# Experts of a recurrent and mixture-of-experts block: gate and up products with the weights stationary, and a second matrix split 128 + 64

## The reference, cut to what matters

```python
topk_w, selected = jax.lax.top_k(softmax(x @ gate.T), 8)
flat_experts = selected.reshape(-1)
gather_indices = jnp.argsort(flat_experts, stable=True)
x_perm = x[gather_indices // 8]                                   # 16384 rows of 256
first_gemm = ragged_dot(x_perm, swapaxes(gate_up_proj, 1, 2), token_counts)      # 256 -> 384
intermediate = silu(first_gemm[:, :192]) * first_gemm[:, 192:]
second_gemm = ragged_dot(intermediate, swapaxes(down_proj, 1, 2), token_counts)  # 192 -> 256
unperm = zeros_like(second_gemm).at[gather_indices].set(second_gemm)
out = (unperm.reshape(-1, 8, 256) * topk_w[..., None]).sum(axis=1)
```

## Time and profile before

| | us |
|---|---|
| time, median of 3 runs (lowest to highest) | 2985.74 (2984.24 to 2986.35) |
| the profiled execution's own time | 2986.55 |
| its span, first to last instruction | 2985.2 |
| experts' stage, first L902 to last L939 | 2169.7 to 2625.5 |

### The profile page before, as it was taken

How to read it: one execution, slowest core, us unless ns; L and a number is a source line. 1 busy time by engine, 2 the same in 40 slices (tenths; PEclk the granted TensorE clock), 3 DMA queues, 4 the chain that set the end, 5 groups by cost and what they waited for, 6 DMA issues and landing times.

```text
span 2985.2 us, 150990 instructions
## 1 busy us (share of the span) xinstructions
PE 2734.0 (92%) x59732; PEld 2284.0 (77%) x59732; DVE 2077.2 (70%) x12188; ACT 1613.8 (54%) x8443; POOL 338.9 (11%) x457
## 2 busy tenths in 40 slices
PE   7689999999999999999999999998679999979984
PEld 4478999989989899998999989878556666744331
DVE  6688888877777777777777777665456666665238
ACT  3445555566666666666666666543335555511115
POOL 0000101101001010010100101001024444410000
PEclk7555555555555555555555555555589999979997
DMA  3142323212123221231212312101568665251000
GB/s 132 39 118 84 98 73 93 88 38 82 59 75 97 61 83 58 76 92 59 85 55 76 95 57 89 32 14 45 211 222 259 196 193 170 74 175 53 1 0 28
DMA packets 170143, 270.95 MB, mean 91 GB/s; under 512 B 23353, under 2 KB 125644, under 8 KB 167140
## 3 DMA queue, kind: packets, MB, share of 16 engines
q1 hardware_dynamic: 125524, 202.29, 21.6%
q0 software_dynamic: 15312, 33.67, 3.3%
q10 hardware_dynamic: 28608, 25.35, 3.1%
HBM read 170.77 MB, written 98.70 MB: 90 GB/s over the span
## 4 chain that ended last, share of the span: by engine, by line
PE 84%; DVE 8%; ACT 4%; issue 2%; DMA 1%; SPq 0%; POOL 0%; POOLq 0%; ACTq 0%; DVEq 0%
PE work L678 9%; PE bank_h L688 7%; PE bank_r L688 7%; PE bank_z L688 7%; PE bank_g L688 7%; PE bank_h L697 5%; PE work L688 5%; PE bank_r L697 4%; PE bank_z L697 3%; PE bank_g L697 3%; PE work L914 3%; PE bank_z L914 3%; PE bank_h L939 2%; PE work L939 2%; PE work L1025 2%
## 5 line engine op out<-in xcount | busy, mean ns | idle before, releaser
L688 PEld LDWEIGHTS work<-h_run,hi_r 128*128 128x128 f16 x4092 | 258.3, 119 | 164.8 <-DVE h_run L1783 150.0
L688 PE MATMUL work<-h_run,hi_r 128*128 128x2 f16 x4092 | 286.8, 174 | 65.3 <-DVE h_run L1783 60.9
L1783 DVE TENSOR_TENSOR_SCAN h_run<-z_run,hh_run 128x12 f16<-128x12 f32 x1024 | 186.8, 182 | 229.3 <-ACT hh_run L1224 210.5
L1224 ACT ACTIVATE hh_run<-bank_h 128x4 f32<-128x4 f32 x1024 | 179.2, 175 | 275.7 <-PE bank_h L697 275.0
L1205 ACT ACTIVATE r_guess<-work 128x4 f32<-128x4 f32 x1023 | 177.0, 173 | 236.0 <-PE work L688 218.7
L1768 DVE TENSOR_TENSOR_SCAN rh_run<-r_run,h_run 128x12 f16<-128x12 f32 x1023 | 187.1, 183 | 151.5 <-ACT r_run L1214 107.9
L688 PE MATMUL bank_g<-h_hi,hi_g 128*128 128x2 f16 x4092 | 253.4, 166 | 38.7 <-ACT h_hi L1194 38.1
L697 PE MATMUL bank_h<-rh_run,hi_h 128*128 128x2 f16 x4092 | 263.8, 169 | 1.8 <-DVE rh_run L1768 1.2
L1219 ACT ACTIVATE z_run<-bank_z 128x4 f32<-128x4 f32 x1024 | 180.3, 176 | 149.1 <-PE bank_z L697 4.2
L688 PE MATMUL bank_h<-h_run,hi_h 128*128 128x2 f16 x4092 | 253.7, 166 | 3.3 <-DVE h_run L1765 3.3
L697 PE MATMUL bank_g<-h_lo,hi_g 128*128 128x2 f16 x4092 | 253.2, 166 | 1.4 <-DVE h_lo L1746 0.5
(11 more groups left out here) (481 smaller groups left out, 8076.8 us busy)
## 6 DMA issues: line engine op xcount, KB each, us to landing
stage<-in_gate_up SPq DMA_DIRECT2D x128, 384.0 KB
stage<-in_down SPq DMA_DIRECT2D x128, 192.0 KB, 3.0
gu_split<-parts SPq DMA_DIRECT2D x64, 384.0 KB, 2.8
gu_ring<-gu_split SPq DMA_DIRECT2D x64, 384.0 KB
xt<-x_rows ACTq DMA_DIRECT2D x191, 128.5 KB, 2.2
x_rows<-zero_rows SPq DMA_DIRECT2D x64, 257.0 KB, 3.3
yk<-y_rows SPq DMA_DIRECT2D x16, 1024.0 KB, 4.8
dn_split<-parts SPq DMA_DIRECT2D x64, 192.0 KB, 2.7
```

What stands on the lines that cost most here:

```text
L688: ins = pe.matmul(o[:, m, step, :], w[:, k, m * P:(m + 1) * P], hi(k), start=False, stop=False, skip_group_check=True)
L1224: act.activation(two(t.hh_run[:, :, 1]), gate_in(t.h, c2, s2), ACT.Tanh, scale=scale_of["h"]).then_inc(s.hh_act, 1)
L1783: dve.tensor_tensor_scan(t.h2_run[:, 0:3 * KH * B], threes(t.z_run), threes(t.hh_run), 0.0, ALU.mult, ALU.add).then_inc(s.h2hi, 1)
```

## The change

1. **Gate and up.** The weights of the ring become the stationary operand, the turned rows the streamed one. The product comes out with the inner features on the partitions. 384 outputs make three blocks of 128 columns of the bank, so there are 18 matmuls of 128 streamed columns in place of 6 of 384. The host orders the outputs so that block 0 is gate 0:128, block 1 is up 0:128, and block 2 has up 128:192 in its first 64 rows and gate 128:192 in its last 64.
2. **The transposes of `mid`, ACT's copy `midT` and their turn of the loop go**; the loop runs to `NTILES + 1`, and the second matrix is applied in turn i - 2.
3. **ACT** makes `silu` in two instructions; the second reads rows 64:128 of block 2 and writes rows 0:64. **DVE** makes one multiply of 256 columns to single precision, a copy to half precision, and the difference; rows 64:128 of `silu`'s second half stay zero from two memsets.
4. **Second matrix**: 128 and 64 rows of contraction in place of 96 and 96, still six matmuls of 256 streamed columns. Each transfer of an odd piece (stage, split store, ring) becomes two.

```diff
@@ tensor_experts
-    for i in range(NTILES + 3):
+    for i in range(NTILES + 2):
...
-            for q, (a, b) in enumerate(PRODUCTS):
-                for k in range(KH):
-                    w = t.gu_ring[:, bass.ds(slot_of[n], 1), a, k, :].rearrange("p a n -> p (a n)")
-                    ins = pe.matmul(bank[:, 0:2 * INTER], t.xtT[n % 2][:, b, k], w, start=(q == 0 and k == 0),
-                                    stop=(q == 2 and k == KH - 1))
+            for m in range(3):
+                for q, (a, b) in enumerate(PRODUCTS):
+                    for k in range(KH):
+                        w = t.gu_ring[:, bass.ds(slot_of[n], 1), a, k, m * P:(m + 1) * P].rearrange("p a n -> p (a n)")
+                        ins = pe.matmul(bank[:, m * P:(m + 1) * P], w, t.xtT[n % 2][:, b, k], start=(q == 0 and k == 0),
+                                        stop=(q == 2 and k == KH - 1), skip_group_check=True)
             ins.then_inc(s.gu_mm, 1)
...
         n = i - 2
-        if 0 <= n < NTILES:
-            bank = tile_banks(t, n)[2].bitcast(FP16)
+        if n >= 0:
+            bank = tile_banks(t, n)[3]
             pe.wait_ge(s.mid, n + 1)
             if n >= 2:
-                pe.wait_ge(s.midT, n - 1)
-            for part in range(2):
-                for j in range(2):
-                    at = (2 * part + j) * P
-                    ins = pe.transpose(bank[0:HI, at:at + P], t.mid[n % 2][:, part, j * HI:(j + 1) * HI], t.identh)
-            ins.then_inc(s.mid_turned, 1)
-        n = i - 3
...
                 pe.wait_ge(s.yt, n - 1)
-            for q, (a, b) in enumerate(PRODUCTS):
-                for j in range(2):
-                    w = t.dn_ring[:, bass.ds(slot_of[n], 1), a, j, :].rearrange("p a n -> p (a n)")
-                    ins = pe.matmul(bank[:, 0:D], t.midT[n % 2][:, b, j], w, start=(q == 0 and j == 0),
-                                    stop=(q == 2 and j == 1))
+            for j, rows in enumerate((slice(0, P), slice(0, REST))):
+                for q, (a, b) in enumerate(PRODUCTS):
+                    w = t.dn_ring[rows, bass.ds(slot_of[n], 1), a, j, :].rearrange("p a n -> p (a n)")
+                    ins = pe.matmul(bank[:, 0:D], t.mid[n % 2][rows, b, j * P:(j + 1) * P], w, start=(j == 0 and q == 0),
+                                    stop=(j == 1 and q == 2))
             ins.then_inc(s.tiles_done, 1)
@@ scalar_experts
-            act.activation(t.silu[n % 2], tile_banks(t, n)[1][:, 0:INTER], ACT.Silu, scale=t.gu_down).then_inc(s.silu, 1)
+            if n >= 2:
+                act.wait_ge(s.mid, n - 1)
+            act.activation(silu[:, 0:P], bank[:, 0:P], ACT.Silu, scale=t.gu_down)
+            act.activation(silu[0:REST, P:2 * P], bank[REST:P, 2 * P:3 * P], ACT.Silu,
+                           scale=t.gu_down[REST:P]).then_inc(s.silu, 1)
         n = i - 2
-        if 0 <= n < NTILES:
-            act.wait_ge(s.mid_turned, n + 1)
-            if n >= 2:
-                act.wait_ge(s.tiles_done, n - 1)
-            act.copy(t.midT[n % 2].rearrange("p a j n -> p (a j n)"),
-                     tile_banks(t, n)[2].bitcast(FP16)[0:HI, 0:4 * P]).then_inc(s.midT, 1)
@@ vector_experts
-            dve.scalar_tensor_tensor(t.mid[n % 2][:, 0], up, t.gu_mid, t.silu[n % 2], ALU.mult, ALU.mult)
-            v.on(dve.scalar_tensor_tensor(t.mid32[n % 2], up, t.gu_mid, t.silu[n % 2], ALU.mult, ALU.mult))
+            v.on(dve.scalar_tensor_tensor(mid32, tile_banks(t, n)[1][:, P:3 * P], t.gu_mid, t.silu[n % 2], ALU.mult,
+                                          ALU.mult))
             dve.wait_ge(v.sem, v.n)
-            dve.tensor_tensor(t.mid[n % 2][:, 1], t.mid32[n % 2], t.mid[n % 2][:, 0], ALU.subtract).then_inc(s.mid, 1)
+            if n >= 2:
+                dve.wait_ge(s.tiles_done, n - 1)
+            v.on(dve.tensor_copy(mid[:, 0], mid32))
+            dve.wait_ge(v.sem, v.n)
+            dve.tensor_tensor(mid[:, 1], mid32, mid[:, 0], ALU.subtract).then_inc(s.mid, 1)
@@ sync_program
     def fetch_expert(e):
...
-        sp.dma_start(t.dn_ring[:, e % RING].rearrange("p j k n -> p (j k n)"), t.dn_split[e]).then_inc(expert_sem(s, e), 16)
+        sp.dma_start(t.dn_ring[:, slot, :, 0], dn[0:P]).then_inc(expert_sem(s, e), 16)
+        sp.dma_start(t.dn_ring[0:REST, slot, :, 1], dn[P:INTER]).then_inc(expert_sem(s, e), 16)
```

More of the change, by code:

```diff
@@ L40 @@
 NT = NTC * P
-HI = INTER // 2
+REST = INTER - P
 RING = 6
@@ L113 @@
     count_mm table_in table_mm row_table table_sb tiles_done experts_ready tile_ready
-    x_turned xT gu_mm silu mid mid_turned midT yt
+    x_turned xT gu_mm silu mid yt
     tl0 tl1 tl2 tl3 tl4 tl5 tl6 tl7 tl8 tl9 tl10 tl11
@@ L403, in place_tiles @@
                 t.xtT = [sb(f"xtT{i}", [P, 2, KH, P], FP16) for i in range(2)]
[L404 to L407, removed]
+                t.silu = [sb(f"silu{i}", [P, 2 * P]) for i in range(2)]
+                t.mid32 = [sb(f"mid32_{i}", [P, 2 * P]) for i in range(2)]
+                t.mid = [sb(f"mid{i}", [P, 2, 2 * P], FP16) for i in range(2)]
                 t.yt = [sb(f"yt{i}", [P, D]) for i in range(NB)]
@@ L457 @@
 chunk_rows = lambda h2: h2.rearrange("p t (k b) three -> p k t b three", k=KH)[:, :, :, :, 2]
-piece_rows = lambda q: P if q % 2 == 0 else HI
 piece_cols = lambda q: KH * 2 * INTER if q % 2 == 0 else 2 * D
+slice_rows = lambda q, i: slice(0, REST if (q % 2, i) == (1, 1) else P)
 slice_cols = lambda i: slice(i * SLICE, (i + 1) * SLICE)
-piece_view = lambda t, q: t.stage[q % NSTAGE][0:piece_rows(q), 0:piece_cols(q)]
+piece_view = lambda t, q: t.stage[q % NSTAGE][:, 0:piece_cols(q)]
+moves = lambda q: 16 * (1 + q % 2)
 stage_sem = lambda s, q: (s.stage0, s.stage1, s.stage2, s.stage3)[q % NSTAGE]
 store_sem = lambda s, q: (s.store0, s.store1, s.store2)[q % NSPLIT]
-stores_before = lambda q: len([p for p in range(NPIECE, q) if p % NSPLIT == q % NSPLIT])
+stores_before = lambda q: sum(moves(p) for p in range(NPIECE, q) if p % NSPLIT == q % NSPLIT)
 expert_sem = lambda s, e: (s.ex0, s.ex1, s.ex2, s.ex3, s.ex4, s.ex5)[e % RING]
@@ L509, in fetch_piece @@
             sp.wait_ge(s.split, q - NPIECE - NSTAGE + 1)
-        src = A["gate_up" if q % 2 == 0 else "down"][q // 2 % NE].rearrange("(k p) n -> p k n", p=piece_rows(q))
-        sp.dma_start(piece_view(t, q).rearrange("p (k n) -> p k n", k=KH), src).then_inc(stage_sem(s, q), 16)
+        if q % 2 == 0:
+            sp.dma_start(piece_view(t, q).rearrange("p (k n) -> p k n", k=KH),
+                         halves(A["gate_up"][q // 2 % NE])).then_inc(stage_sem(s, q), 16)
+        else:
+            src = A["down"][q // 2 % NE]
+            sp.dma_start(piece_view(t, q)[:, 0:D], src[0:P]).then_inc(stage_sem(s, q), 16)
+            sp.dma_start(piece_view(t, q)[0:REST, D:2 * D], src[P:INTER]).then_inc(stage_sem(s, q), 16)
     sp.wait_ge(s.d0, len(D0))
@@ L520, in sync_program @@
             sp.wait_ge(s.split, q - NPIECE + 1)
-            dst = (t.gu_split if q % 2 == 0 else t.dn_split)[q // 2 % NE].rearrange("p (j n) -> p j n", j=2)
-            sp.dma_start(dst, t.parts[q % NSPLIT][0:piece_rows(q), :, 0:piece_cols(q)]).then_inc(store_sem(s, q), 16)
+            parts, e = t.parts[q % NSPLIT], q // 2 % NE
+            if q % 2 == 0:
+                sp.dma_start(t.gu_split[e].rearrange("p (j n) -> p j n", j=2), parts).then_inc(store_sem(s, q), 16)
+            else:
+                dst = t.dn_split[e].rearrange("p (j n) -> p j n", j=2)
+                sp.dma_start(dst[0:P], parts[:, :, 0:D]).then_inc(store_sem(s, q), 16)
+                sp.dma_start(dst[P:INTER], parts[0:REST, :, D:2 * D]).then_inc(store_sem(s, q), 16)
     def fetch_expert(e):
-        sp.dma_start(t.gu_ring[:, e % RING].rearrange("p j k n -> p (j k n)"), t.gu_split[e]).then_inc(expert_sem(s, e), 16)
-        sp.dma_start(t.dn_ring[:, e % RING].rearrange("p j k n -> p (j k n)"), t.dn_split[e]).then_inc(expert_sem(s, e), 16)
+        slot, dn = e % RING, t.dn_split[e].rearrange("p (j n) -> p j n", j=2)
+        sp.dma_start(t.gu_ring[:, slot].rearrange("p j k n -> p (j k n)"), t.gu_split[e]).then_inc(expert_sem(s, e), 16)
+        sp.dma_start(t.dn_ring[:, slot, :, 0], dn[0:P]).then_inc(expert_sem(s, e), 16)
+        sp.dma_start(t.dn_ring[0:REST, slot, :, 1], dn[P:INTER]).then_inc(expert_sem(s, e), 16)
     for q in range(2 * NPIECE, 2 * NPIECE + NSPLIT):
-        sp.wait_ge(store_sem(s, q), 16 * stores_before(q))
+        sp.wait_ge(store_sem(s, q), stores_before(q))
     for e in range(RING):
@@ L543, in sync_program @@
     for e in range(RING):
-        sp.wait_ge(expert_sem(s, e), 32)
+        sp.wait_ge(expert_sem(s, e), 48)
         sp.sem_inc(s.experts_ready, 1)
@@ L1152, in split_hi @@
     def split_hi(q, i):
-        p, cols = piece_rows(q), slice_cols(i)
+        p, cols = slice_rows(q, i), slice_cols(i)
         if i == 0:
@@ L1158, in split_hi @@
             if stores_before(q):
[L1159 to L1162, removed]
+                act.wait_ge(store_sem(s, q), stores_before(q))
```

(14 more changed lines are left out.)

29 lines of the change are left out of this document (13 added, 16 removed).

## The result

The changed kernel takes 3133.74 us (median of 4 runs, 3132.44 to 3135.18) for 2985.68 us before on the same chip: ratio 1.0498, 95% interval 1.0485 to 1.0511. The forecast was 3155 us in a range of 3120 to 3215. The profiled execution has a span of 3131.1 us for 2985.2.

What follows compares the result with a forecast made beforehand. TensorE's instruction stream sets the tile at 2.288 us, array 2.09. Terms 1.00 + 0.05 - 0.125 = +0.925 a tile over 186 tiles, +172.0 - 2 - 1 = +169 us: forecast 3155 us, range 3120 to 3215.

Steps and rivals of the forecast that it cites:

- Gate and up, +1.00: TensorE's stream at gate and up: eight more address computations a tile at 0.125 us each, +1.00 us a tile.
- +0.05: Gate and up: four more matmul pairs without an address computation, taken as 0.05 us a tile, between 0 and 0.23.
- Transposes of `mid`, -0.125: Between gate and up and second matrix: dropping the transposes saves 0.125 us a tile, bounds 0 and 0.25.
- Second matrix, 0: Second matrix: six matmuls and four address computations a tile stay, so no change in time.
- T's 1.91: Instruction-stream theory's array work a tile in e2's expectation: 22 x 0.057 + 6 x 0.109 = 1.91 us.
- Array, ACT, DVE: nothing: Experts' tiles: array, ACT and DVE work stays hidden, with a chain of some 2.4 us to finished `mid`; cost 0.
- DMAs, 0: Odd pieces' transfers made in two, 256 issues on SP, far below its wait before the experts: cost 0.
- How many tiles: Experts' stage: five of 191 tiles cost nothing during the wait for layer 3's weights; 186 tiles pay, +172.0 us.
- A: Experts' stage: the clock falls to half and the array sets the tile, +281 us, 3267 us; chance 0.06.
- B: Gate and up: each of the 18 matmuls computes its address, 1.625 us more a tile, 3285 us; chance 0.03.
- C: Gate and up: block offset needs no computation, 2962 us, or 3014 at 0.081 us a pair; chance 0.05, 0.04 faster.
- D: Changed transfers or recurrences: something there slows the kernel, no size given; chance 0.02.

Runs made afterwards that it cites:

- e3: Changed kernel, but all three gate-and-up blocks read block 0's weights, so 18 matmuls have four addresses: 2984.68 us, ratio 1.0001 to the kernel before.
- e6: Kernel before without the bounds check behind the slot's load: 3028.38 us for 3059.19 on a second chip, ratio 0.990.
- e2: Changed kernel, but gate and up read a fixed copy of expert 0's weights, without address computations: 2981.18 us, ratio 0.9985 to the kernel before.
- e1: Kernel before with only gate and up cut into three blocks of 128 columns, rows still stationary: 3163.36 us, ratio 1.060.
- e4: Changed kernel with the next slot's load moved behind the second matrix, to the turn's end: 3147.75 us, ratio 1.0545 to the kernel before.
- e7: Changed kernel without the bounds check behind the slot's load: 3158.81 us on the second chip, ratio 1.0325 to the kernel before.
- e5: Kernel before with each transfer of an expert's second matrix made in two: 3056.11 us for 3059.19 on the second chip, ratio 0.9991.

## Why the prediction was right, step by step

- **The bound.** "The stream is the one that sets the tile" was argued from 2.288 us against an array of 2.09. E6 shows it: 0.286 us off the stream takes 0.18 off the tile, down to the array.
- **Gate and up, +1.00.** Right in cause and size. 12 computations a tile are counted. Fewer of them give it back (e3 with four, e2 with none), and in the old orientation they cost the same (e1). In the trace they start 0.130 to 0.133 us apart on average, 0.124 at the median, whether or not a pair without a computation lies between: eight are 1.05. The pairs themselves add nothing. That the +0.05 set apart for them fits is luck: it comes from 0.131 in place of 0.125.
- **Transposes of `mid`, -0.125.** e1 minus the changed kernel gives 0.14.
- **Second matrix, 0.** Right for the stream: four computations for six matmuls, as before. The array needs 0.19 us more a tile for the changes of rows, which the prediction did not see. In the changed kernel this is hidden; it is about half of what e2 and e3 stay above T's 1.91.
- **Slot's load: the term that was missing.** The prediction took it as unchanged. From its start to the next instruction's are 0.445 us on average before and 0.360 after (from the starts of all in the stage), -0.085. The sum is then 1.05 - 0.125 - 0.085 = 0.84, and measured are 3.120 - 2.287 = 0.833 for the forecast's 0.925. Over 186 tiles this is 17 us. Why the load is shorter is open: it is long in the kernel before, in e3 and in e4, short in e1, e6 and e7. E6 has it at the same place in the tile as the kernel before, and e3 at the same as the changed kernel.
- **Array, ACT, DVE: nothing.** Right: no wait of the loads is for ACT or DVE, and the array's 2.1 us lie well below 3.12. The chain was put at some 2.4 us and is 2.2 (e2).
- **DMAs, 0.** Right inside the stage. Before it the two transfers took away most of one stop of 3.8 us, and the experts were reached some 5.5 us earlier, of which e5 against e6 shows 5.2. The prediction had nothing for this.
- **How many tiles.** Five again run ahead of the wait for layer 3's weights, and that wait takes their extra time in:

```profile
2165.93 2.13 PE L930 MATMUL bank_z<-xtT,gu_ring 128*128 128x128 f16 x18
...
2180.08 1.43 PE L930 MATMUL bank_z<-xtT,gu_ring 128*128 128x128 f16 x18
...
2187.14 2.29 DVE L1856 TENSOR_REDUCE wm<-W 128x1 f32<-128x2048 f32 x1 [6.80 <-DMA W<-in_W]
...
2189.90 2.15 PE L930 MATMUL work<-xtT,gu_ring 128*128 128x128 f16 x18 [6.58 <-DVE xtT L1889]
```

- **The sum.** The profiled executions differ by 3132.44 - 2986.55 = 145.9 us. The forecast's 169, less 17 for the tile (nearly all of it the slot's load) and 6 ahead of the stage, is 146. The two misses point the same way and do not cancel.
- **Rivals.** A: the clock stayed at 1.00 with the array at work 1.89 of 3.12 us (22 x 0.056 + 6 x 0.109). B: 2292 computations and not 3438. C: not 764; its 2962 and 3014 us leave out the 3 us that the forecast takes off at the start and the end of the stage. D: the recurrences did move, by some 5.5 us, but to the faster side. The 0.081 us a pair of the Trainium skill ("TensorE: Matmul & The Clock Gate", section "Back-to-back issue gap") doesn't hold here: e2's 18 pairs follow each other every 0.056 us.

## What to carry to other kernels

Where operands sit at addresses known only at run time, count the different addresses and not the matmuls or the columns: the stream pays for each, and long matmuls hide what short ones lay bare. A busy share of 98% does not show which of array and stream sets the pace. The pitch of starts does, together with a cause of "issue"; that cause alone does not, since the 0.21 us at a change of rows bear the same name. A change that saves columns or transposes can lose if it cuts long products into short ones with addresses of their own.

## What the runs showed of the hardware that had not been expected

- The load of a register from SBUF took 295 to 297 ns at the least in each of these kernels, and 301 to 352 ns at the median. The changed kernel and e4 differ by 14 us in 191 tiles with it. What makes it longer is not shown.
- A matmul that follows one with another number of rows (64 after 128, 128 after 64) started about 0.2 us after it, for 0.109 without the change. With 96 rows followed by 128 the kernel before shows no such wait.
- The check of a loaded value's bounds costs 0.286 us of the stream each time: 31 us in the kernel before, about 53 in the changed one.
- TensorE's stream stopped once for 2.7 to 3.8 us in the recurrence, just after the fetches of six experts were issued; with smaller transfers it stopped for 0.2 to 1.2 us.
